# The last weight matmul of a per-node step, cut to 64 of 128 rows and paired across the halves of the array

## The reference, cut to what matters

```python
w = jnp.einsum('nd,dkio->nkio', embedding, weight)      # D = 16, K = 3
b = jnp.einsum('nd,do->no', embedding, bias)
As = [eye(N), A, 2.0 * (A @ A) - eye(N)]
x_g = jnp.einsum('knm,bmc->bnkc', jnp.stack(As, 0), x)
out = jnp.einsum('bnki,nkio->bno', x_g, w) + b
x = _layernorm(x + out)
```

## Time and profile before

| what | value |
|---|---|
| median of 3 runs | 1294.76 us (1294.4 to 1295.26) |
| the profiled execution, its own time | 1295.21 us |
| its span, first to last instruction | 1293.3 us |
| PE busy | 1258.5 us, 97% |
| DVE busy | 729.9 us, 56% |
| the T matmuls (L703) | 1280, from 121.6 to 621.6 us |

### The profile page before, as it was taken

One profiled execution on the slowest core, in us unless ns is written; L12 is line 12 of the kernel. 1 busy time (PEld: TensorE's weight loads), 2 busy tenths in 40 slices (PEclk: granted clock), 3 DMA queues, 4 the chain that ended last, 5 costly groups with the idle time before them and its releaser, 6 DMA issues.

```text
span 1293.3 us, 16451 instructions
## 1 busy us (share of the span) xinstructions
PE 1258.5 (97%) x6048; PEld 1045.5 (81%) x6048; DVE 729.9 (56%) x1811; ACT 239.8 (19%) x427; POOL 62.0 (5%) x52
## 2 busy tenths in 40 slices
PE   5999999999999999999999999999999999999996
PEld 5887878787878787778888888888888888888875
DVE  4724898777767777778624443351256245434524
ACT  5622101120111201120112121121111121221211
POOL 0000000000000000000001001000000010010000
PEclk9999999999999999999999999999999999999998
DMA  9712112111121210101000000010001000000000
GB/s 361 290 65 85 26 53 72 43 61 37 54 61 37 59 33 20 54 21 42 14 1 1 2 1 1 1 62 5 1 24 43 1 1 1 2 1 1 33 1 35
DMA packets 27509, 55.08 MB, mean 43 GB/s; under 512 B 3472, under 2 KB 14224, under 8 KB 24976
## 3 DMA queue, kind: packets, MB, share of 16 engines
q1 hardware_dynamic: 27424, 53.96, 12.2%
HBM read 41.89 MB, written 12.06 MB: 42 GB/s over the span
## 4 chain that ended last, share of the span: by engine, by line
PE 92%; DVE 5%; ACT 1%; issue 1%; DMA 1%; SPq 0%; DVEq 0%; ACTq 0%
PE ps L594 28%; PE ps L595 28%; PE ps L703 20%; PE ps L612 7%; PE ps L633 2%; PE ps L634 2%; PE ps L606 2%; DVE nat L958 1%; DVE ring L958 1%; DVE xs L868 1%; PE ps L623 1%; ACT xs L736 1%; DMA b0t<-in_b 0%; DVE sml L900 0%; DVE sml L891 0%
## 5 line engine op out<-in xcount | busy, mean ns | idle before, releaser
L594 PE MATMUL ps<-B,xs 128*128 128x512 f32 x1664 | 658.2, 396 | 6.0 <-DVE xs L868 3.7
L595 PE MATMUL ps<-B,xs 128*128 128x512 f32 x1664 | 649.9, 391 | 0.0
L594 PEld LDWEIGHTS ps<-B,xs 128*128 128x128 f32 x1664 | 312.7, 188 | 71.1 <-issue 4.3
L595 PEld LDWEIGHTS ps<-B,xs 128*128 128x128 f32 x1664 | 312.8, 188 | 63.9
L703 PE MATMUL ps<-Tw,xs 128*128 128x512 f32 x1280 | 316.6, 396 | 2.2 <-DVE ring L958 2.2
L703 PEld LDWEIGHTS ps<-Tw,xs 128*128 128x128 f32 x1280 | 238.1, 187 | 61.4 <-DVE ring L958 4.2
L856 DVE TENSOR_TENSOR ring<-ps,rrep 128x512 f32<-128x512 f32 x94 | 64.5, 689 | 286.0 <-PE ps L595 270.0
L958 DVE SCALAR_TENSOR_TENSOR nat<-ps,embn,nat 128x128 f32<-128x128 f32 x448 | 153.7, 343 | 55.8 <-PE ps L703 55.6
L958 DVE SCALAR_TENSOR_TENSOR ring<-ps,embn,ring 128x128 f32<-128x128 f32 x512 | 175.2, 342 | 0.0
L612 PEld LDWEIGHTS ps<-W,ring 128*128 128x128 f32 x896 | 110.4, 191 | 8.0 <-DVE ring L856 3.6
L612 PE MATMUL ps<-W,ring 128*128 128x128 f32 x896 | 113.2, 275 | 2.3 <-DVE ring L856 2.3
(11 more groups left out here) (65 smaller groups left out, 623.1 us busy)
## 6 DMA issues: line engine op xcount, KB each, us to landing
raw<-in_at SPq DMA_DIRECT2D x15, 1024.0 KB, 17.2
ring<-in_xn SPq DMA_DIRECT2D x16, 256.0 KB, 2.9
ring_x<-in_xt SPq DMA_DIRECT2D x32, 128.0 KB, 3.2
ring_x<-y1d SPq DMA_DIRECT2D x32, 128.0 KB, 3.4
out<-nat SPq DMA_DIRECT2D x16, 256.0 KB, 2.1
y1d<-ring SPq DMA_DIRECT2D x14, 256.0 KB, 2.7
zd<-nat SPq DMA_DIRECT2D x12, 256.0 KB, 3.1
nat<-zd SPq DMA_DIRECT2D x3, 1024.0 KB, 4.8
```

The costliest lines, as they stand in the source:

```text
L594: pe.matmul(bank, x[:, 0, m, :], of, start=m == 0, stop=False)
L595: mm = pe.matmul(bank, x[:, 1, m, :], of, start=False, stop=ends and m == NT - 1)
```

## The change

In a T step the first four matmuls of batch 0 and of batch 1 are issued as before. The fifth of each batch then follows in a loop of its own, behind those eight: it reads only the 64 rows of S that hold the high part, and the same 64 rows of plane 3 of `Tw`. These are rows 0 to 63 for batch 0 and rows 64 to 127 for batch 1, so the two last matmuls lie in different halves of the array's rows and write different banks. The product low x low, which the whole S by plane 3 contained, is no longer computed. The number of matmuls and of weight loads stays at ten for each step, and the last one raises `s_T`.

```diff
                         for q in range(2):
                             at_k = slice(q * 256 + kk * P, q * 256 + (kk + 1) * P)
                             H, Lo = st[:, 2 * half, at_k], st[:, 2 * half + 1, at_k]
                             S = st[:, 4 + 2 * (c % 2) + q, k * P:(k + 1) * P]
-                            seq = [(H, 0), (H, 1), (Lo, 0), (S, 2), (S, 3)]
-                            for i, (src, wi) in enumerate(seq):
-                                mm = pe.matmul(ps[:, 4 + 2 * p + q, :], src, Tw[:, wi, 512 * p:512 * p + 512],
-                                               start=i == 0, stop=i == 4)
+                            for i, (src, wi) in enumerate([(H, 0), (H, 1), (Lo, 0), (S, 2)]):
+                                pe.matmul(ps[:, 4 + 2 * p + q, :], src, Tw[:, wi, 512 * p:512 * p + 512],
+                                          start=i == 0, stop=False)
+                        for q in range(2):
+                            S, hi = st[:, 4 + 2 * (c % 2) + q, k * P:(k + 1) * P], halves(q)[0]
+                            mm = pe.matmul(ps[:, 4 + 2 * p + q, :], S[hi, :], Tw[hi, 3, 512 * p:512 * p + 512],
+                                           start=False, stop=True)
                         mm.then_inc(s_T, 1)
```

## The result

The changed kernel takes 1311.8 us (median of 4 runs, 1311.23 to 1312.61) against 1294.62 us for the kernel before: a ratio of 1.0132, 95% interval 1.0115 to 1.015. The change costs 17 us. I had forecast 1273 us, with 1266 to 1308 as the range; the time lies above it, close to rival A's 1307.

A forecast was written before the change was run, and what follows sets the result against it. PE's stream was taken as the bound: 128 steps x 0.213 us = 27.3 us, 0.86 of it on the path = 23.6, less 2 for DVE = 21.6 us gained, giving 1273 us; range 1266 to 1308 us.

The forecast's parts named there:

- rival A: At each switch between full matmuls and halves the array empties: a step 0.109 us longer, 1307 us; chance 0.28.
- What bounds the kernel: In the T-step stretches PE's stream sets the end, in places DVE's; 86% of T matmul time on the path.
- (1): Batch 0's fifth matmul moved behind batch 1's first four: no cost, the same ten matmuls.
- (2): Last matmuls of 64 rows instead of 128: no gain from the rows themselves.
- (3): The two halves of a T step stream together, the second 0.02 us behind: 0.213 us saved for a step.
- rival B: The second half of a pair starts 0.11 us late: 0.10 us saved for a step, 1284 us; chance 0.17.
- rival C: The halves run in turn, each at a pitch of its own: 1294.8 us; chance 0.10.
- (4): Switching from full array to halves and back, twice a step: taken as zero, upper ends 0.161 and 0.27 us.
- DVE as the next bound: In the first T-step stretch DVE is late next, so 2 us were taken off the gain.

The follow-up runs named there:

- run 1: Changed kernel with the two last matmuls at full height (128 rows), still together at the end of the step: 1294.7 us, ratio 1.000.
- run 2: Changed kernel with both 64-row matmuls reading rows 0 to 63, the same half of the array: 1337.2 us.
- run 3: Changed kernel without batch 1's 64-row matmul, batch 0's kept, nine matmuls for a step: 1311.4 us.
- run 5: Changed kernel with the pair of halves issued twice in a row in each step: 1336.6 us.
- run 6: Changed kernel with each 64-row matmul right behind its own batch's four full ones, four switches for a step: 1387.9 us.
- run 4: Changed kernel with both 64-row matmuls left out, eight full-height matmuls for a step: 1252.4 us.
- run 8: As run 7, with adjacency quarters given out only after every second T step (coarser weave): 1297.2 us, ratio 1.0018 to the kernel before.
- run 12: Against run 7: a tile's four halves in one island, behind the p = 0 step's full matmuls, old weave: 1297.2 us, ratio 1.0017 to the kernel before.
- Run 9: Kernel before, ten full-height matmuls for a step, with only the coarser weave of run 8: 1300.2 us.
- run 7: Changed kernel with the p = 1 step issuing its halves first, so neighbouring steps' four halves form one island: 1307.7 us.
- run 10: As run 8, with the number of quarters given out for pairs 1 and 2 rounded up to an even one: 1297.5 us.
- run 11: Kernel before, ten full-height matmuls for a step, with the even weave of run 10: 1298.6 us.
- run 13: Against the kernel before, each tile's form chosen by its surroundings: 18 merged, 32 with an island, 14 all full-height: 1294.7 us, ratio 0.9995.

## Why the prediction was wrong

*What bounds the kernel* was right: PE's stream sets the end. 19 us more of PE time became 16 us in the stretch, 84% where the prediction used 86%.

*(1) Order, no cost*: right, shown by run 1.

*(2) Fewer rows make nothing cheaper*: right in the loads, 183 ns against 188, and shown in the matmul by run 2, where a half behind another in the same rows costs a full pitch of 0.23 us.

*(3) Overlap*: right, and even a little better than taken. Run 3 puts the second half's cost at nothing, and run 5 shows a pair in 0.23 us, where I had 0.02 us on top. The figure of the Trainium skill in (3), starts some 4 ns apart, is what the trace shows: in its recorded starts, which the printed rows round to 10 ns, the second half is 3 or 4 ns behind the first in all 128 pairs. Rivals B and C fall.

*(4) "I take zero here"* is the step that failed. A switch costs 0.19 us each way, above the 0.161 us of an array that empties and below the 0.27 us with an exposed load. The starts split it: the halves start 0.33 us behind the last full matmul, 0.09 us over a pitch; the next full one starts 0.42 us behind them, 0.19 over, which is 0.10 us by which the halves' exposed load delays them and 0.09 us for the border again; and the full one behind that is late by another 0.10 us, by its neighbour's exposed load. So both terms are there; the exposed load has the size that I gave it (0.11), and the emptying is smaller than 0.161 because the load starts 0.07 us before the row ahead ends. No run changes one of the two without the other. Two of them are 0.39 us, against 0.23 us gained: a step is 0.15 us longer, not 0.21 us shorter. I took zero because a return from L612 showed no emptying. That row was a change of the number format at full height. Its load started with the last L612 (0.002 us behind it in the recorded starts), as in a stream, and 0.11 us of matmul was too short to hide 0.19 us of load. It said nothing of a change of rows; it was the nearest row in time and not in kind. Runs 1, 5 and 6 show that the price goes with the switches: none with no switch, the same with two pairs in an island, double with two islands.

*Rival A* described what happened, at 0.109 us a step where 0.15 was measured. With 0.15 its sum is 0.86 x 128 x 0.15 = 16.5 us, 1311.3 us, and 1311.8 was measured. The rule of the Trainium skill that the prediction cited beside A, that a change of the tiling mode drains the engine, agrees with the trace: loads are held back at every border, for 0.37 us in front of a pair. I gave it 0.28. The rule was explicit, nothing in the trace spoke to the same case, and that should have made A the likeliest.

*DVE as the next bound* in the stretch of pair 0 could not be seen with the change, since PE became slower; run 4 shows it, where 19 of 78 us did not reach the end, most of them by waits on DVE.

## What to carry to other kernels

Two 64-row matmuls in different halves of the array do run in the time of one, but going to the half mode and back cost 0.39 us here, 1.7 matmuls of 512 columns. One pair among full-height matmuls loses 0.15 us; an island saves PE time from two pairs on (0.85 us against 0.93 for four full matmuls), though no run here turned that into a kernel that is measurably faster than the one before. So gather the pairs before using it, and only where that makes nobody wait. When a rule of the Trainium skill speaks to the case and the nearest row is of another kind, the rule's case deserves the larger chance.

## What was not expected of the hardware

A wait of PE of 2.2 to 2.5 us can cost more than itself: the granted clock fell to 0.50 behind it in runs 8 and 12, and 1.7 us of clock went missing each time. It is not the length of the wait alone that decides. In run 3 the clock fell behind a wait of 1.6 us. Run 9 has two waits of 2.47 us on the scaling: behind the one that ends at 287.43 us the granted clock of 288 to 290 us was 0.50, behind the one that ends at 427.89 us it stayed at 1.00. And the idle 2.2 us in front of the first product behind the branch (L594 at 101.77 us before, at 100.35 in the changed kernel) left the clock at 1.00 in the profiled execution of before and was followed by 0.50 in that of the changed kernel:

```profile
103.00:105.00 2.00, 2.00 (x6) 1.52 (x5) 0.00 (x0) 0.00 (x0) 0.00 (x0) 0.50 0.71 291
```

The T steps begin only at 122 us, at 121.8 in the one and 122.0 in the other, so this is no part of the change's 16 us. It is a matter of one or two microseconds from execution to execution, about the size of what runs 7 to 13 were to resolve.
